# A two-layer recurrent kernel: routing by batch, up products in three fp32r passes, the scan's left operand by DMA

## The chip, the cores and the metric

The kernel runs on one core of a Trainium2 chip. The metric is the device time of one execution in microseconds (us), the median of several runs. Five engines work side by side: TensorE (PE, weight loads shown as PEld), VectorE (DVE), ScalarE (ACT), GpSimd (POOL) and SyncE (SP), which issues all DMAs here. Order between engines is kept by semaphores that the program names.

## The reference, cut to what matters

The input x is 4 batches x 512 tokens x 128 channels, all in fp32. Layer 0 normalises it (LayerNorm), computes a linear attention branch and a mixture-of-experts branch, multiplies the two (silu of the second) and adds the product to x. Layer 1 does the same with a pairwise scan as its attention branch and a second mixture of experts.

```python
# layer 0 gate: 32 experts in 4 groups, 2 groups stay, 8 experts taken
scores = sigmoid(logits); choice = scores + bias
group score = sum of the two best in a group; mask = the 2 best groups
topk_idx = top 8 of where(mask, choice, 0); w = scores[topk]; w = w / (w.sum + 1e-20) * 2.5
# layer 1 scan over tokens, d = 1, 2, 4, ..., 256
shifted = concat([identity] * d, x[:, :-d])
v = (shifted + x) @ W                       # W = polar factor of W_scan_raw
att = softmax(q k^T / sqrt(32)) over 4 lanes per token, q = shifted, k = x
x = shifted + rms_norm(att @ v) / (1 + lane)
# layer 1 experts: 8 of width 512, 2 taken
relu(x @ w1[e] + b1[e]) @ w2[e] + b2[e]
```

## The kernel before, in words

Every engine has one program, written out by hand, and instructions of an engine run in its order. Tokens lie on partitions (token layout, 4 tiles of 128 tokens per batch) or channels do (channel layout, 128 x 512 per batch).

Prologue. VectorE does LayerNorm (`layer_norm` L1123, `normalise` L1135), TensorE transposes to channels and makes the router's logits for all 16 token tiles, ScalarE copies `xnT` and a rounded `xnT_hi` out and takes the sigmoid (L924). GpSimd splits the gate and up weights of layer 0 into two fp32r parts (`split_weights` L368) and makes the remainder `xnT_lo` (L373). VectorE routes all 16 tiles in one chain of small steps (L1160 to L1224): MAX8 per group, comparisons of group scores, MAX8 and match-replace, weights, and three bf16 parts of them (`gate0_parts`). TensorE transposes these (`gates_to_rows` L609) for all batches, then the loop begins.

Layer 0 loop. For each batch b and each pair p of experts (16 pairs), TensorE does `gate_up` (L583: six fp32r passes of 512 columns, high x low, high x high, low x high, for gate and for up), `gate_rows` (one bf16 product that spreads the gates), `down` of two pairs earlier (fp32), and `extras` (L689): attention products, the steps of a polar iteration that makes W, the transposes of layer 1's input. VectorE does `routed_hidden` (L1226, two multiplications, L1230 and L1235) and its `extras` (L1291), among them `polar_step`, `attention_stats` at p = 11, `gate_tokens` at p = 4. `h0` is a ring of three.

Crossing. VectorE finishes layer 0 for batch 3 and normalises it, TensorE transposes it, does `scan_input` (L682), then `router_logits` (L744, layer 1, all tiles), then `values` of the first slot. VectorE does `routing1` (L1321) behind its first slot.

Scan. 9 levels x 4 batches = 36 slots, k = 0 to 35. In each slot:
- TensorE: `state_channels` of the next slot (L767, 4 transposes of x_tok), `values` (L783, (left + x) W), the first half of `expert_down` of one block of layer 1's experts, `left_tokens` of the next slot (L775, 4 transposes), the second half, and four `expert_up` products of the next block (L792, fp32, 512 columns each, with w1 loaded from memory per expert). Bank 3 serves up products 0 and 3.
- ScalarE: `state_in` (L1019, copies the state in channel layout into xT, which has 256 columns of the identity ahead of it, and from there a copy shifted by d columns, leftT), `values_out`, `left_out` (L1027, from bank 1 to left_tok), `expo`, `square`, four `relu`, `rsqrt`.
- VectorE: `products` (L1357, left from bank 1), `scores` (L1369), `add_lanes` (L1363), `score_max`, `softmax_shift`, four accumulations of expert output (L1404), `square_sum` (L1383), `exp_sum`, `mix_values` (L1392).
- GpSimd: `halve_mix` (L469), `rms_factor` (L477), `scale_z` (L481), `new_state` (L488, writes x_tok of two slots back), `sum_inputs` (L444, leftT + xT of the next slot), `last_product` (L451), `last_mix` (L460).
SyncE loads w1 and w2 of the next expert behind semaphores.

Tail. In slot 33 TensorE also does `gated_biases` (L750); then come the last slots, the gating of the state, projections and the output.

## Time and profile before

| what | value |
|---|---|
| median of 3 runs | 631.2 us (624.67 to 637.21) |
| the profiled execution, its own time | 631.67 us |
| its span (first to last instruction) | 630.0 us |
| TensorE busy / VectorE / ScalarE / GpSimd | 563.2 / 507.2 / 282.2 / 377.2 us |
| mean granted TensorE clock | 0.95 |
| HBM traffic | 9.50 MB read, 1.05 MB written |

Times in rows are microseconds from the span's start. An instruction's row gives its start, its duration, its engine and line, what it writes and reads, and in brackets how long its engine had been idle and what ended that. TensorE rows of an fp32 product come in two entries each. PEclk is the granted TensorE clock, 1.00 being full speed. Lines L524 and L527 are TensorE's helpers for a product and a transpose.

### The profile page before, as it was taken

To read this page: it belongs to the slowest core of one execution; us is meant where nothing else is said; L and a number is where in the kernel's file an instruction comes from. 1 tells how busy PE (TensorE), PEld (TensorE's weight loads), DVE (VectorE), ACT (ScalarE), POOL (GpSimd) and SP (SyncE) were. 2 spreads that over 40 slices of the span, in tenths; PEclk is the share of its full clock that TensorE was granted. 3 is DMA by queue.
4 is the path that set the end of the run, shared out by engine and by line. 5 is a ranking of instruction groups with operands and counts; after the bars stand their busy time and mean duration, and the time that the engine had idled before them with its cause. 6 is when DMAs were issued, how large, how long until landed. Compare 5 with 4: busy or idle time off the path is not lost.

```text
span 630.0 us, 9276 instructions
## 1 busy us (share of the span) xinstructions
PE 563.2 (89%) x2934; PEld 405.8 (64%) x2934; DVE 507.2 (81%) x922; ACT 282.2 (45%) x640; POOL 377.2 (60%) x347
## 2 busy tenths in 40 slices
PE   4949999999999995889999999999999999997854
PEld 3735666666666664767767667667677676675724
DVE  7584565664765764599999999999999999999775
ACT  3612242242252244154654655645645546555332
POOL 6930010030030033339999998998999999989754
PEclk9987999999999998689999999999999999999677
DMA  8300000000000000000100000010000100000002
GB/s 255 116 2 0 2 0 2 0 1 0 2 0 2 2 0 0 1 1 2 34 0 17 17 8 25 0 33 0 17 17 0 33 0 17 17 1 0 2 0 68
DMA packets 12185, 10.87 MB, mean 17 GB/s; under 512 B 1784, under 2 KB 10624, under 8 KB 11776
## 3 DMA queue, kind: packets, MB, share of 16 engines
q1 hardware_dynamic: 12160, 10.55, 5.4%
q8 instruction: 13, 0.21, 0.1%
q14 instruction: 12, 0.10, 0.1%
HBM read 9.50 MB, written 1.05 MB: 17 GB/s over the span
## 4 chain that ended last, share of the span: by engine, by line
DVE 38%; PE 36%; issue 17%; ACT 5%; POOL 2%; DMA 0%; DVEq 0%; ACTq 0%; POOLq 0%
PE bank L524 34%; DVE bank L1369 10%; DVE shared L1357 9%; DVE shared L1363 7%; ACT shared L1043 3%; PE bank L527 2%; DVE shared L1392 2%; DVE shared L1377 1%; DVE ssum L1387 1%; DVE smax L1373 1%; POOL shared L469 1%; ACT shared L1041 1%; DVE z_ms L1383 1%; DVE shared L1404 1%; DVE ln_stats L1126 1%
## 5 line engine op out<-in xcount | busy, mean ns | idle before, releaser
L524 PE MATMUL bank<-xnT,w 128*128 128x512 f32 x256 | 121.1, 608 | 5.6 <-ACT shared L1055 5.6
L524 PE MATMUL bank<-w,shared 128*128 128x128 f32 x1024 | 125.1, 275 | 0.0
L524 PEld LDWEIGHTS bank<-w,shared 128*128 128x128 f32 x1024 | 119.9, 193 | 0.0
L469 POOL TENSOR_TENSOR shared<-shared 128x1024 f32<-128x1024 f32 x36 | 85.3, 2368 | 25.9 <-DVE shared L1392 25.8
L524 PE MATMUL bank<-shared 128*128 128x512 f32 (+3 forms) x280 | 89.3, 444 | 0.0
L1230 DVE TENSOR_TENSOR shared<-shared,bank 128x512 f32<-128x512 f32 x64 | 44.0, 687 | 55.9 <-PE bank L524 49.5
L935 ACT ACTIVATE shared<-bank 128x512 f32<-128x512 f32 x68 | 40.5, 598 | 97.6 <-PE bank L524 93.4
L1369 DVE TENSOR_REDUCE bank<-shared 128x64 f32<-128x2048 f32 x36 | 82.6, 2295 | 1.2
L524 PEld LDWEIGHTS bank<-xnT,w 128*128 128x128 f32 x256 | 43.9, 192 | 59.6 <-issue 35.5
L1055 ACT ACTIVATE shared<-bank,b_now 128x512 f32<-128x512 f32 x128 | 80.5, 679 | 1.4 <-ACT b_now L1073 1.2
L444 POOL TENSOR_TENSOR shared<-shared,xT 128x512 f32<-128x512 f32 x36 | 60.1, 1670 | 17.7 <-ACT shared L1025 17.7
L524 PE MATMUL bank<-xnT_lo,wgu_hi 128*128 128x512 f32 x136 | 63.7, 468 | 2.8 <-DVE xT L1158 2.8
L524 PEld LDWEIGHTS bank<-shared 128*128 128x128 f32 x280 | 51.2, 198 | 22.6 <-issue 17.3
L1357 DVE TENSOR_TENSOR shared<-bank,x_tok 128x1536 f32<-128x1536 f32 x36 | 63.1, 1752 | 2.9 <-ACT shared L1029 2.7
L1392 DVE TENSOR_TENSOR shared<-shared,bank 128x1536 f32<-128x1536 f32 x36 | 62.8, 1745 | 0.0
L524 PE MATMUL bank<-polar_x,shared 128*128 128x128 f32 x288 | 44.4, 302 | 20.4 <-DVE shared L1392 19.6
L1363 DVE TENSOR_TENSOR shared<-shared 128x512 f32<-128x512 f32 x36 | 60.6, 1682 | 0.4 <-POOL shared L469 0.4
L524 PEld LDWEIGHTS bank<-polar_x,shared 128*128 128x128 f32 x288 | 38.7, 208 | 27.3 <-issue 27.3
L524 PE MATMUL bank<-xnT_hi,wgu_lo 128*128 128x512 f32 x136 | 54.1, 398 | 0.0
L524 PE MATMUL bank<-xnT_hi,wgu_hi 128*128 128x512 f32 x136 | 53.7, 395 | 0.0
L416 POOL TENSOR_SCALAR xn<-x,ln_mv,ln_rstd 128x128 f32<-128x128 f32 x12 | 9.4, 793 | 66.3 <-ACT ln_rstd L888 66.3
L451 POOL TENSOR_TENSOR shared<-shared,x_tok 128x512 f32<-128x512 f32 x36 | 45.6, 1268 | 5.5 <-ACT shared L1029 5.5
(179 smaller groups left out, 915.4 us busy)
## 6 DMA issues: line engine op xcount, KB each, us to landing
w<-in_w SPq DMA_DIRECT2D x32, 64.0 KB, 1.8
w<-in_w SPq DMA_DIRECT2D x8, 256.0 KB, 2.7
shared<-in_wd SPq DMA_DIRECT2D x1, 1088.0 KB, 12.5
x<-in_x SPq DMA_DIRECT2D x4, 256.0 KB, 3.5
shared<-in_wg SPq DMA_DIRECT2D x1, 1024.0 KB, 8.2
shared<-in_wu SPq DMA_DIRECT2D x1, 1024.0 KB, 10.2
out<-x SPq DMA_DIRECT2D x4, 256.0 KB, 2.3
shared<-in_attn_w SPq DMA_DIRECT2D x1, 384.0 KB, 3.7
```

The costliest lines, as they stand in the source:

```text
L444: g.tensor_tensor(sumT[:, b], leftT[:, b], xT[:, b, PAD:PAD + N], ALU.add).then_inc(s("sum_done"), 1)
L451: g.tensor_tensor(prod[:, b % 2, :, :, LANES - 1], left_tok[:, b].rearrange("p j (l d) -> p j l d", l=LANES), x_tok[:, b, :, (LANES - 1) * ...
L469: g.tensor_tensor(mix2[:, b % 2].rearrange("p j l m d -> p (j l) (m d)"), mix[:, b % 2, :, :, 0:2].rearrange("p j l m d -> p (j l) (m d)") ...
L524: return nc.tensor.matmul(out, lhsT, rhs, start=start, stop=stop)
L935: a.activation(silu_g[:, i % 2], bank[G[i % 2]][:], ACT.Silu).then_inc(s("silu_done"), 1)
L1043: a.activation(z_sq[:, b % 2, :, :, 0:LD], z[:, b % 2].rearrange("p j (l d) -> p j l d", l=LANES), ACT.Square).then_inc(s("zsq_done"), 1)
L1055: a.activation(hT[:, c], bank[UP[c]][:], ACT.Relu, bias=b1_now[:, c:c + 1]).then_inc(s("ffn_relu"), 1)
L1230: tt(silu_gu[:, i % 2], silu_g[:, i % 2], bank[U[i % 2]][:], ALU.mult).then_inc(s("gu_done"), 1)
L1357: tt(prod[:, b % 2, :, :, 0:LANES - 1], left.broadcast_to([P, TB, LANES, LANES - 1, LD]), right.broadcast_to([P, TB, LANES, LANES - 1, LD] ...
L1363: tt(z[:, b % 2].rearrange("p j (l d) -> p (j l) d", l=LANES), m[:, :, 0], m[:, :, 1], ALU.add).then_inc(s("z_done"), 1)
L1369: v.tensor_reduce(score[:, b % 2], prod[:, b % 2], AX_X, ALU.add).then_inc(s("score_done"), 1)
L1392: tt(mix[:, b % 2, :, :, 0:LANES - 1], sexp[:, b % 2, :, :, 0:LANES - 1].unsqueeze(4).broadcast_to([P, TB, LANES, LANES - 1, LD]), values. ...
```

## The change

Routing by batch. ScalarE takes exp(-logits) instead of the sigmoid; VectorE adds 1 and takes the reciprocal. The chain stands in four functions for one batch: `route_groups`, `route_masks`, `route_best`, `route_weights`, 20 steps. Batch 0 goes ahead of the loop, mixed with the shared expert's products; batch b + 1 goes into the loop of batch b at p = 3, 7, 9 and 10, its gates are transposed at p = 13. The loads of the first four units of wg and wu go ahead of the attention weights, and GpSimd splits them first. The shared expert's first two blocks on TensorE go ahead of the token sums.

Up products. w1 of all experts is loaded in one DMA into the room of the layer 0 weights once these are split. GpSimd splits it expert by expert (`split_expert`) into the units of `wgu_hi` and `wgu_lo` that the last batch has used; ScalarE makes `xnT_hi` of layer 1's input, GpSimd the remainder (`token_rest1`). `expert_up` is three fp32r passes. VectorE's and GpSimd's scan waits until all eight experts are split. w2 has two buffers.

Scan. x_tok becomes tiles 1 to 4 of `state_ext`, whose tile 0 is the identity. SyncE moves the state down by d tokens into left_tok with two DMAs per slot (`shift`). `sum_inputs` adds left_tok and x_tok in token layout; TensorE transposes the sum (`sum_channels`, between up products 1 and 2), ScalarE copies it out (`sum_in`, between `rsqrt` and `relu` 2). `left_out` copies left_tok into bank 1 for `products`. `state_channels`, `left_tokens`, `state_in` and the padding of xT are gone. The loops over levels on TensorE, ScalarE, GpSimd and SyncE are written out.

```diff
+            sp.dma_start(polar_x[:], scan_raw_d).then_inc(s("ld_scan"), 16)
+            sp.dma_start(wg[:, 1:5], wg_d[:, 1:5]).then_inc(s("ld_next"), 16)
+            sp.dma_start(wu[:, 1:5], wu_d[:, 1:5]).then_inc(s("ld_next"), 16)
...
+            sp.wait_ge(s("w_lo_done"), 6)
+            sp.dma_start(w1, w1_d.rearrange("e p (u m) h -> p e u m h", m=2)).then_inc(s("ld_w1"), 16)
+            def shift(k):
+                b, d = k % B, 1 << k // B
+                sp.wait_ge(s("xtok_done"), k + 1)
+                if d < P:
+                    sp.dma_start(left_tok[d:P, b], state_ext[0:P - d, b, 1:TB + 1]).then_inc(s(f"ld_left{b}"), 16)
+                    sp.dma_start(left_tok[0:d, b], state_ext[P - d:P, b, 0:TB]).then_inc(s(f"ld_left{b}"), 16)
+                else:
+                    j = d // P
+                    sp.dma_start(left_tok[:, b, 0:j], state_ext[:, b, 0:1].broadcast_to([P, j, P])).then_inc(s(f"ld_left{b}"), 16)
+                    sp.dma_start(left_tok[:, b, j:TB], state_ext[:, b, 1:TB + 1 - j]).then_inc(s(f"ld_left{b}"), 16)
+            for k in range(LEVELS * B):
+                shift(k)
...
+            def split_expert(e):
+                if e > 0:
+                    pool.wait_ge(s("u_mm"), item((B - 1) * PAIRS + 2 * e) + 1)
+                units = slice(2 * e, 2 * e + 2)
+                raw = w1[:, e].rearrange("p u m h -> p m u h")
+                g.tensor_copy(wgu_hi[:, :, units], raw).then_inc(s("w1_hi_done"), 1)
+                pool.wait_ge(s("w1_hi_done"), e + 1)
+                g.tensor_tensor(wgu_lo[:, :, units], raw, wgu_hi[:, :, units], ALU.subtract).then_inc(s("w1_lo_done"), 1)
             for b in range(B):
                 state_product(b)
+                if b > 1:
+                    token_rest1(b - 2)
                 if b > 0:
                     add_to_x(b - 1)
                     normalise1(b - 1)
                 attention_tokens(b)
+            token_rest1(B - 2)
+            pool.wait_ge(s("ld_w1"), 16)
+            pool.wait_ge(s("u_mm"), item((B - 1) * PAIRS) + 1)
+            for e in range(E1):
+                split_expert(e)
             pool.wait_ge(s("x1_done"), B)
             g.memset(ecmp[:], 0.0).then_inc(s("ecmp_zero"), 1)
             g.memset(acc[:], 0.0).then_inc(s("acc_zero"), 1)
...
+            token_rest1(B - 1)
+            pool.wait_ge(s("w1_lo_done"), E1)
             sum_inputs(0, 0)
             last_product(0, 0)
...
             def sum_inputs(k, b):
-                pool.wait_ge(s("leftT_cp"), k + 1)
-                g.tensor_tensor(sumT[:, b], leftT[:, b], xT[:, b, PAD:PAD + N],
-                                ALU.add).then_inc(s("sum_done"), 1)
+                pool.wait_ge(s(f"ld_left{b}"), 32 * (k // B + 1))
+                pool.wait_ge(s("xtok_done"), k + 1)
+                after(pool, s("state_mm"), k - 1)
+                g.tensor_tensor(sum_tok[:, b % 2], left_tok[:, b], x_tok[:, b], ALU.add).then_inc(s("sum_done"), 1)
...
             def expert_up(e, blk, c):
-                if blk == 0:
-                    pe.wait_ge(s(f"ld_w1_{c}"), e * 16 + 16)
+                if c == 0:
+                    pe.wait_ge(s("x1lo_done"), blk + 1)
+                    pe.wait_ge(s("w1_lo_done"), e + 1)
                 if c == HC - 1:
                     pe.wait_ge(s("ffn_relu"), (e * B + blk) * HC + 1)
-                mm(bank[UP[c]][:], w1[:, c], xnT[:, blk * N:(blk + 1) * N]).then_inc(s("ffn_up"), 1)
+                u, m = 2 * e + c // 2, c % 2
+                tokens = slice(blk * N, (blk + 1) * N)
+                mm(bank[UP[c]][:], wgu_hi[:, m, u], xnT_lo[:, tokens], True, False)
+                mm(bank[UP[c]][:], wgu_hi[:, m, u], xnT_hi[:, tokens], False, False)
+                mm(bank[UP[c]][:], wgu_lo[:, m, u], xnT_hi[:, tokens], False, True).then_inc(s("ffn_up"), 1)
...
             def slot(k, b, this=True, ahead=True, up=None, down=None, then=None):
-                if ahead:
-                    state_channels(k + 1, (b + 1) % B)
                 if this:
                     values(k, b)
                 if down:
-                    expert_down(*down, range(0, TB // 2))
-                if ahead:
-                    left_tokens(k + 1, (b + 1) % B)
-                if down:
-                    expert_down(*down, range(TB // 2, TB))
+                    expert_down(*down, range(TB))
                 if then:
                     then()
                 if up:
-                    for c in range(HC):
-                        expert_up(*up, c)
+                    expert_up(*up, 0)
+                    expert_up(*up, 1)
+                if ahead:
+                    sum_channels(k + 1, (b + 1) % B)
+                if up:
+                    expert_up(*up, 2)
+                    expert_up(*up, 3)
...
-            state_channels(0, 0)
             silu_y_tokens(B - 1)
             tokens_to_channels(B - 1, GB)
-            left_tokens(0, 0)
             scan_input(B - 1, AT)
+            sum_channels(0, 0)
             router_logits()
             slot(0, 0, up=(0, 0))
...
             def left_out(k, b):
-                act.wait_ge(s("left_mm"), k + 1)
-                a.copy(left_tok[:, b].rearrange("p j c -> p (j c)"), bank[1][:]).then_inc(s("left_tok_cp"), 1)
+                act.wait_ge(s(f"ld_left{b}"), 32 * (k // B + 1))
+                after(act, s("prod_done"), k)
+                a.copy(bank[1][:], left_tok[:, b].rearrange("p j c -> p (j c)")).then_inc(s("left_tok_cp"), 1)
...
+            route_groups(0)
+            route_masks(0)
             dve.wait_ge(s("polar_r_done"), 2)
             ts(polar_x[:], polar_x[:], polar_r[:], None, ALU.mult).then_inc(s("polar_x0"), 1)
+            shared_hidden(0)
+            route_best(0)
+            shared_hidden(1)
+            route_weights(0)
...
+                elif p == 3 and b < B - 1:
+                    route_groups(b + 1)
+                elif p == 7 and b < B - 1:
+                    route_masks(b + 1)
+                elif p == 9 and b < B - 1:
+                    route_best(b + 1)
+                elif p == 10 and b < B - 1:
+                    route_weights(b + 1)
...
+            dve.wait_ge(s("w1_lo_done"), E1)
             slot(0, 0, before=False)
             routing1()
```

## Rows read from the trace of the kernel before

**Rows 1.** windows: PE, PEld, DVE, ACT, POOL busy us, then PEclk, DMA share, GB/s.

```profile
34.00:40.00 6.00, 3.20 (x13) 2.37 (x13) 5.90 (x53) 1.20 (x2) 3.79 (x11) 1.00 0.01 3
46.00:56.00 10.00, 8.23 (x25) 4.71 (x24) 4.07 (x7) 2.72 (x5) 0.00 (x0) 0.52 0.00 0
249.00:262.00 13.00, 13.00 (x62) 12.78 (x63) 4.50 (x4) 2.96 (x5) 1.64 (x2) 0.50 0.00 1
350.00:400.00 50.00, 47.75 (x297) 35.71 (x298) 48.92 (x62) 29.11 (x72) 45.99 (x36) 1.00 0.03 10
```

**Rows 2.** timeline of one scan slot: start us, us, engine line op, [idle before it].

```profile
407.45 1.75 DVE L1357 TENSOR_TENSOR shared<-bank,x_tok 128x1536 f32<-128x1536 f32 x1
...
407.61 2.37 POOL L469 TENSOR_TENSOR shared<-shared 128x1024 f32<-128x1024 f32 x1 [0.65 <-DVE shared L1392]
...
411.37 1.27 POOL L488 TENSOR_TENSOR x_tok<-shared 128x512 f32<-128x512 f32 x1
411.44 1.74 DVE L1363 TENSOR_TENSOR shared<-shared 128x512 f32<-128x512 f32 x1
...
412.66 3.72 PE L524 MATMUL bank<-xnT,w 128*128 128x512 f32 x8
...
417.06 1.75 DVE L1357 TENSOR_TENSOR shared<-bank,x_tok 128x1536 f32<-128x1536 f32 x1
```

**Rows 3.** source view of L1363: duration ns min/median/max, first and last start.

```profile
L1363 DVE TENSOR_TENSOR shared<-shared x36: 681/1744/1761, 277.0 to 615.8; 128x512 f32<-128x512 f32 x36
```

**Rows 4.** timeline, layer 0 loop, batch 0, TensorE and VectorE.

```profile
62.03 0.39 PE L524 MATMUL bank<-xnT_hi,wgu_lo 128*128 128x512 f32 x1
...
62.26 0.39 PE L524 MATMUL bank<-xnT_lo,wgu_hi 128*128 128x512 f32 x1
...
78.98 0.69 DVE L1230 TENSOR_TENSOR shared<-shared,bank 128x512 f32<-128x512 f32 x1 [1.15 <-PE bank L524]
...
79.71 0.69 DVE L1235 TENSOR_TENSOR shared<-shared,bank 128x512 f32<-128x512 f32 x1
...
80.31 0.28 DVE L1283 COPY polar_x<-bank 128x128 f32<-128x128 f32 x1
...
85.20 0.31 PEld L524 LDWEIGHTS bank<-shared 128*128 128x128 f32 x2 [0.55 <-DVE shared L1276]
```

**Rows 5.** DMA issues: KB each, median us to landing.

```profile
w<-in_w SPq DMA_DIRECT2D x32, 64.0 KB, 1.8
w<-in_w SPq DMA_DIRECT2D x8, 256.0 KB, 2.7
```

**Rows 6.** timeline, prologue: GpSimd, VectorE and TensorE.

```profile
24.44 2.35 POOL L369 CAST wgu_hi<-shared 128x2048 fp32r<-128x2048 f32 x1
25.07 4.45 DVE L1165 MAX8 shared<-shared 128x8 f32<-128x8 f32 x64
...
26.87 4.63 POOL L371 TENSOR_TENSOR wgu_lo<-shared,wgu_hi 128x2048 fp32r<-128x2048 f32 x1
...
30.96 0.62 DVE L1170 TENSOR_SCALAR polar_x<-polar_x,polar_r 128x128 f32<-128x128 f32 x1
...
45.30 1.09 PE L527 MATMUL bank<-ident_bf,shared 128*96 128x128 bf16 x8 [5.76 <-DVE shared L1224]
...
48.45 0.61 PE L524 MATMUL bank<-gate0T,pair_row 96*128 96x512 bf16 x1 [0.67 <-ACT gate0T L996]
```

**Rows 7.** timeline, crossing from layer 0 into the scan.

```profile
235.34 1.28 POOL L427 TENSOR_TENSOR shared<-shared 128x512 f32<-128x512 f32 x1
...
252.50 6.83 PE L524 MATMUL bank<-gate_w,xnT 128*128 128x8 f32 x32
...
260.07 1.92 PE L524 MATMUL bank<-polar_x,shared 128*128 128x128 f32 x8
...
273.00 1.76 DVE L1357 TENSOR_TENSOR shared<-bank,x_tok 128x1536 f32<-128x1536 f32 x1 [0.22 <-DVE gate L1349]
```

**Rows 8.** timeline, tail: TensorE.

```profile
588.08 7.19 PE L524 MATMUL bank<-b,shared 8*128 8x128 f32 x32 [2.21 <-ACT shared L1015]
```

388 lines of the change are left out of this document (203 added, 185 removed).

## The prediction

> **What bounds the kernel now.** I read the table of windows first, then one stretch of the timeline for each limit it shows. Through the scan stage the vector engine is busy 48.92 of 50 us and TensorE 47.75 [rows 1], so busy shares alone don't say which of them decides. The timeline of one slot does [rows 2]. A slot is one batch's step in one scan level: `products` starts at 407.45 and the next one at 417.06, a period of 9.61 us, and there are 36 slots, 346 us of the 630. The reader is to see where VectorE stands still while it is counted as busy: `add_lanes` (L1363) lasts 1.74 us in the slot, with a fastest of 0.681 and a median of 1.744 over its 36 [rows 3]. It starts at 411.44, 0.07 us behind GpSimd's `new_state` (411.37, 1.27 us), and ends 0.54 us after that ends: it is held until GpSimd is through. So the loop that sets the period goes `mix_values` end (407.5), GpSimd's `halve_mix` to `new_state` (407.61 to 412.64), the 0.5 us that `add_lanes` really needs, then VectorE alone up to the end of the next `mix_values`. The Trainium skill has this in SBUF — State Buffer, section on the shared port: a VectorE instruction with two SBUF inputs and a GpSimd instruction that reads SBUF exclude one another for a whole instruction, and a tensor-scalar form in a two-port mode meets any GpSimd instruction; by that rule the new GpSimd work below costs VectorE too, and the trace agrees (1.744 against 0.681).
>
> The rest of the span: a prologue to 48.45, a layer 0 loop of 4 batches bound by TensorE (about 48.7 us each), a crossing into the scan up to 273.00, and a tail from 588 on.
>
> **Scan slots.** The change takes from TensorE the four transposes of the left operand and swaps each up product for three fp32r passes. In layer 0 such passes start 0.23 us apart [rows 4], three cost 0.69; the fp32 up products take 3.72 us for four with a wait in it [rows 2], some 0.86 each. That is 4 x 0.17 + 0.45 = 1.1 us of TensorE per slot. ScalarE loses two copies and gains one. None of these stands in the loop above. VectorE's program in a slot is unchanged, and GpSimd's six operations are the same in number and size: `sum_inputs` adds two 128x512 tiles in another layout. GpSimd has 0.65 us idle in the slot in any case. I take 0 per slot.
>
> What must hold for the 0: (a) The left operand now comes by two DMAs, started when `new_state` ends (5.2 us into a slot). The copy into PSUM that needs it may be as late as 1.75 us into the next slot, or even some 5 us before `expo` behind it suffers: 6.2 us of cover, 10 at the outside. Loads of 256 KB landed in 2.7 us [rows 5]; no DMA from SBUF to SBUF is in the trace. From 1.8 (64 KB) to twice 2.7 plus two issues it fits; I take 3.5, hidden, and if it took 8 us the slot would grow by 1 to 2. (b) TensorE now waits for `sum_inputs` in the middle of its slot, with up products 2 and 3 behind it: it would stand about 1 us there (6.3 to 7.3 us in), do the transposes and end near 8.8 to 9.3, before the next `mix_values`. (c) ScalarE does `relu` 2 and 3 some 0.6 us later, to 1.2 us into the next slot, when TensorE is just through `values`. (d) The clock: the row of 46 to 56 at 0.52 follows 5.76 us of idleness [rows 6], and in 34 to 40 it kept 1.00 with 3.20 us busy of 6 [rows 1]. With 7.9 of 9.6 us busy I expect 1.00, the upper of its two levels (2.4 GHz; 0.50 is 1.2).
>
> **Prologue.** The router now works for one batch instead of four ahead of the loop: 16 MAX8 instead of 64 (4.45 us, so 1.1) [rows 6], and the 512-wide steps become 128-wide, 0.2 to 0.3 each by the 0.28 us copy [rows 4]. The exp instead of the sigmoid spares a table load. But GpSimd splits weights up to about 32 us, with subtractions as long as 4.63, and VectorE's small steps stop behind them as the polar scaling did (0.62, to 31.58, when the subtraction ended at 31.50) [rows 6]; before, the 64 MAX8 covered that. Step by step: exp at 22.9, first three steps held until 26.8, MAX8 to 28.2, group masks caught by the second subtraction until 32.1 and done at 33.4, shared products and the other steps to 40.9; then TensorE has `gate_up`, `key_values`, `gate_up` and four transposes to do, and the loop begins near 45.2 instead of 48.45 [rows 6]: 3.2 us. TensorE has no 5.76 us gap any more [rows 6], so that the stretch 46 to 56 at clock 0.52 [rows 1] mostly runs at full rate: about 2 to 3 us more, if no new gap is long enough. I take -5.2; ends +2 (held at every step, clock low) and -9.
>
> **Layer 0 loop.** Routing of batches 1 to 3 moves into batches 0 to 2, at p = 3, 7, 9, 10. Sum per batch on VectorE: 1.9 (groups), 1.5 (masks), 1.6 (best), 2.2 (weights: nine steps of 0.25). VectorE has slack of 1.15 us per pair (its wait before 78.98), and the ring on top. The first three bursts fit. The last doesn't: after `h0` at 79.71 to 80.40 it moves the `polar_x` copy from 80.31 to 82.6, the next pair's products to 83, and the batch-norm and polar steps of p = 11 behind them; TensorE already waits 0.55 us for that polar step (85.20) [rows 4]. I get 1.7 us of wait per batch, 5.1, plus 3 x 0.45 for the gate transposes that now stand in the loop: +6.5. Ends: +1.4 (all hidden) and +12 (each burst costs its 1.5 us excess).
>
> **Crossing into the scan.** This is the largest term. The up products need w1 split into two fp32r parts, for 8 experts, on GpSimd, and the program puts this behind `attention_tokens` of batch 3, which ends at 236.6 [rows 7]. A cast of 2048 columns took 2.35 and a subtraction 4.63 [rows 6], so 512 columns cost 0.65 and 1.25, with the handshakes 2.1 per expert, 16.9 us for 8. Then GpSimd's order is: one activation remainder (to 238.7), the eight splits (255.6), some 2 us given away to VectorE's layer norm, the memsets (2.75), the last remainder (1.3), and only then `sum_inputs` 0 and with it TensorE's first transposes, near 263. In the old kernel that addition was long done, and TensorE did `router_logits` from 252.50, 6.83 us at clock 0.50, and ended `values` at 262 [rows 1, 7]. Now `router_logits` stands behind the transposes: 264 to 271, `values` to 273, first `mix_values` to 275.5, `routing1` 7.5 us as before, slot 1 at 282.7 instead of 273.00: +9.6. Ends: +3 (splits at the rate of one 1.27 us operation each) and +14 (each VectorE step held).
>
> **Tail.** In the last level `gated_biases` takes TensorE 7.19 us [rows 8]. The sum's transposes and ScalarE's copy of them now stand between it and `values`, where before there was only the state's transpose: +1.1; ends 0 and +3.
>
> **Sum**, against the profiled execution, 631.7 us (span 630.0, 1.7 around it; the median of the runs shown is 631.2): 631.7 - 5.2 + 6.5 + 0 + 9.6 + 1.1 = 643.7. The ends of the terms give 627 and 663; they won't all fall on one side, so this case's own range is 635 to 654.
>
> **Rivals.**
> Order at the port turned round, the case on the other side: not slower. The 0.07 us between `new_state` and `add_lanes` is all that decides who goes first. If anything lets `add_lanes` go first, it takes 0.68 instead of 1.74, and the slot is bound by GpSimd instead: 9.61 less its idle 0.65, plus the 0.2 us by which `new_state` waits longer, 9.2 us. That is 0.4 x 35 = -14, so 629.7. It decides from a shift of 0.1 us. For it: new ScalarE and DMA traffic. Against it: VectorE's and GpSimd's instructions up to that point are identical, and both start from the same event.
> Splits and bursts cheap: prologue -8, loop +1.4, crossing +3, tail 0: 628. For it: VectorE's small steps may slip between GpSimd's. Against it: the serial order on GpSimd and the 0.62 us row.
> A wait in the slot: the shift lands late, or `relu` 3 holds the down products, or GpSimd's sum meets VectorE elsewhere. 0.4 us per slot are 14 us: 658.
> The clock falls in the scan because TensorE now idles 1.7 us per slot: 7.9 us of work become up to 15, a period of some 14 us: above 780. The row of 34 to 40 at 1.00 speaks against it.
> A rule of the Trainium skill that speaks about this change is in DMA: Bandwidth & Descriptors, on the cost of a transfer: about 2 us fixed plus the bytes over 436 GB/s, so an estimate of 2.6 us for 256 KB. By that the shift is hidden and the sum stands; the 2.7 us row is a load from HBM and agrees, a copy inside SBUF no row here shows.
>
> **How the numbers follow.** Forecast 0.54, port order 0.14, cheap splits 0.14, wait in the slot 0.14, clock 0.04. About 2% is what a measurement of this kernel can tell from no change, so slower begins at 643.8, nearly on the forecast: half of it, plus the last two cases, is 0.45; faster (under 618.6) needs the port order together with the cheap splits, or a gain that I don't see: 0.13; the rest, 0.42, is within 2%. The range of 80% takes in the lower rivals and most of the wait: 624 to 660.
>
> **What would show it.** Right: slot period 9.61 and L1363 at 1.74 in the timeline; the eight splits in one block from about 238 to 256 on GpSimd; TensorE idle until about 263, slot 1 at 282 to 283; the loop's start near 45; TensorE waits of 1 to 2 us near p = 11 and 12 of batches 0 to 2; clock 1.00 in the scan. Wrong: L1363 at 0.68; a copy to PSUM that waits for a DMA; `sum_inputs` 0 before 258; a scan clock under 1.

## The result, and the profile after

The changed kernel takes 639.1 us (median of 4 runs, 638.2 to 639.4); the kernel before took 630.1 in the runs beside it (4 runs, 624.7 to 637.2). The ratio is 1.0141, with a 95% interval of 1.0097 to 1.0186: slower by about 1.4%. The 637.2 is a slow execution, and the ratios here and below compare fast ones only. The profiled execution took 638.2 us, its span is 636.5 us instead of 630.0.

Where the 6.5 us of span come from is read by four marks that both timelines have: the first `h0` of layer 0's loop, its last, the `products` of slot 1, and the `products` of slots 34 and 35. The lengths between them, each a difference of two starts, in us:

| stretch | before | after | difference |
|---|---|---|---|
| start to the first `h0` | 49.16 | 43.92 | -5.24 |
| first to last `h0` | 189.13 | 193.10 | +3.97 |
| last `h0` to slot 1 | 34.71 | 42.73 | +8.02 |
| slot 1 to slot 34 (33 slots) | 317.00 | 317.55 | +0.55 |
| slot 34 to 35 | 14.87 | 13.99 | -0.88 |
| the rest | 25.13 | 25.21 | +0.08 |

Start with the scan, the longest part. The windows of the kernel after, in the same stretches and with the same columns as [rows 1]:

```profile
34.00:40.00 6.00, 4.22 (x17) 2.87 (x17) 5.42 (x25) 2.28 (x4) 1.55 (x6) 1.00 0.82 307
46.00:56.00 10.00, 9.33 (x35) 5.45 (x34) 7.62 (x28) 2.19 (x4) 0.92 (x2) 1.00 0.00 1
249.00:262.00 13.00, 7.29 (x32) 6.60 (x32) 5.09 (x6) 2.87 (x5) 12.41 (x11) 0.50 0.11 35
350.00:400.00 50.00, 42.61 (x300) 36.56 (x299) 48.95 (x62) 24.86 (x64) 46.13 (x38) 1.00 0.12 33
```

In 350 to 400 TensorE is busy 42.61 us instead of 47.75 and ScalarE 24.86 instead of 29.11: the work did leave them, 1.0 and 0.8 us per slot. VectorE (48.95) and GpSimd (46.13) stand as before, and so does the period. The timeline of one slot, which answers [rows 2]:

```profile
405.16 1.75 DVE L1437 TENSOR_TENSOR shared<-bank,state_ext 128x1536 f32<-128x1536 f32 x1
405.32 2.36 POOL L512 TENSOR_TENSOR shared<-shared 128x1024 f32<-128x1024 f32 x1 [0.60 <-DVE shared L1472]
405.39 1.13 PE L569 MATMUL bank<-polar_x,shared 128*128 128x128 f32 x8 [0.85 <-DVE shared L1472]
...
409.06 1.27 POOL L531 TENSOR_TENSOR state_ext<-shared,left_tok 128x512 f32<-128x512 f32 x1
409.14 1.74 DVE L1443 TENSOR_TENSOR shared<-shared 128x512 f32<-128x512 f32 x1
...
410.29 1.75 POOL L488 TENSOR_TENSOR shared<-left_tok,state_ext 128x512 f32<-128x512 f32 x1
...
412.10 0.66 PE L572 MATMUL bank<-ident,shared 128*128 128x128 f32 x4 [0.61 <-POOL shared L488]
...
414.76 1.75 DVE L1437 TENSOR_TENSOR shared<-bank,state_ext 128x1536 f32<-128x1536 f32 x1
```

From one `products` (L1437) to the next are 9.60 us. `new_state` (L531) starts 0.08 us ahead of `add_lanes` (L1443), which lasts 1.74, as in [rows 2]. What is new is how long TensorE stands still: 0.85 us ahead of `values`, where it was 0.48 before, and 0.61 for the sum, where it did not wait. Its time was turned into waiting.

Then the crossing, which answers [rows 7]: GpSimd's splits (the first and last shown, eight casts and eight subtractions in all), its first sum, and TensorE behind it.

```profile
237.07 0.61 POOL L460 CAST wgu_hi<-shared 128x512 fp32r<-128x512 f32 x1
...
251.50 1.27 POOL L462 TENSOR_TENSOR wgu_lo<-shared,wgu_hi 128x512 fp32r<-128x512 f32 x1
...
256.59 1.26 POOL L488 TENSOR_TENSOR shared<-left_tok,state_ext 128x512 f32<-128x512 f32 x1
...
257.90 1.11 PE L572 MATMUL bank<-ident,shared 128*128 128x128 f32 x4 [4.39 <-POOL shared L488]
258.81 6.83 PE L569 MATMUL bank<-gate_w,xnT 128*128 128x8 f32 x32
265.49 2.06 PE L569 MATMUL bank<-polar_x,shared 128*128 128x128 f32 x8
```

The router's 6.83 us were done from 252.50 before [rows 7]; now they begin 6.3 us later, at the same low clock (0.50). Slot 1 begins at 279.75 instead of 273.00.

### The profile page after: what moved, and what is told of

It reads as the page before. It is cut to its first block, busy times and chain, and to the rows that moved or that the text cites. A ratio compares the mean times of both kernels' runs of the same rounds, so it can differ in the third digit from the quotient of the medians.

```text
span 636.5 us, 8860 instructions
## 1 busy us (share of the span) xinstructions
PE 532.1 (84%) x2918; PEld 410.6 (65%) x2918; DVE 525.6 (83%) x993; ACT 261.9 (41%) x607; POOL 397.3 (62%) x367
## 4 chain that ended last, share of the span: by engine, by line
DVE 40%; PE 31%; issue 17%; ACT 5%; POOL 5%; DMA 0%; DVEq 0%; ACTq 0%; POOLq 0%
PE bank L569 30%; DVE shared L1437 9%; DVE bank L1449 9%; DVE shared L1443 7%; ACT shared L1094 3%; DVE shared L1472 2%; PE bank L572 2%; POOL wgu_lo L462 1%; DVE shared L1457 1%; DVE ssum L1467 1%; ACT shared L1092 1%; DVE shared L1302 1%; DVE smax L1453 1%; DVE shared L1307 1%; POOL wgu_hi L460 1%
## 5 line engine op out<-in xcount | busy, mean ns | idle before, releaser
L569 PE MATMUL bank<-xnT_lo,wgu_hi 128*128 128x512 f32 x264 | 121.1, 459 | 8.7 <-ACT shared L1106 6.9
L569 PE MATMUL bank<-w,shared 128*128 128x128 f32 x1024 | 121.1, 277 | 0.0
L569 PE MATMUL bank<-xnT_hi,wgu_lo 128*128 128x512 f32 x264 | 105.7, 400 | 0.0
L569 PE MATMUL bank<-xnT_hi,wgu_hi 128*128 128x512 f32 x264 | 105.3, 399 | 0.0
L1437 DVE TENSOR_TENSOR shared<-bank,state_ext 128x1536 f32<-128x1536 f32 x36 | 63.0, 1750 | 5.4 <-ACT bank L1080 5.1
L569 PEld LDWEIGHTS bank<-xnT_lo,wgu_hi 128*128 128x128 f32 x264 | 50.9, 193 | 19.9 <-ACT shared L1106 8.9
L1088 ACT ACTIVATE shared<-shared 128x64 f32<-128x64 f32 x36 | 9.2, 256 | 130.8 <-DVE shared L1457 130.8
L488 POOL TENSOR_TENSOR shared<-left_tok,state_ext 128x512 f32<-128x512 f32 x36 | 61.6, 1712 | 0.0
L572 PE MATMUL bank<-ident,shared 128*128 128x128 f32 x180 | 32.7, 306 | 34.4 <-POOL shared L488 24.5
L1443 DVE TENSOR_TENSOR shared<-shared 128x512 f32<-128x512 f32 x36 | 59.7, 1658 | 0.3 <-POOL shared L512 0.3
L569 PEld LDWEIGHTS bank<-xnT_hi,wgu_lo 128*128 128x128 f32 x264 | 50.5, 191 | 11.8
```

Source lines behind the costliest of these rows:

```text
L488: g.tensor_tensor(sum_tok[:, b % 2], left_tok[:, b], x_tok[:, b], ALU.add).then_inc(s("sum_done"), 1)
L569: return nc.tensor.matmul(out, lhsT, rhs, start=start, stop=stop)
L572: return nc.tensor.transpose(out, in_, ident[:] if idm is None else idm)
L1437: tt(prod[:, b % 2, :, :, 0:LANES - 1], left.broadcast_to([P, TB, LANES, LANES - 1, LD]), right.broadcast_to([P, TB, LANES, LANES - 1, LD] ...
L1443: tt(z[:, b % 2].rearrange("p j (l d) -> p (j l) d", l=LANES), m[:, :, 0], m[:, :, 1], ALU.add).then_inc(s("z_done"), 1)
```

## The experiments

Twelve kernels ran. Eleven are made from the kernel after and one from the kernel before. All are read by the same marks (us; "slots" is slot 1 to slot 34):

| kernel | first `h0` | loop | crossing | slots | slot 34 | span |
|---|---|---|---|---|---|---|
| before | 49.16 | 189.13 | 34.71 | 317.00 | 14.87 | 630.0 |
| after | 43.92 | 193.10 | 42.73 | 317.55 | 13.99 | 636.5 |
| 1 fp32 up products | 44.03 | 192.80 | 38.92 | 317.73 | 13.43 | 632.2 |
| 2 router first | 43.25 | 194.41 | 39.03 | 316.29 | 15.31 | 633.3 |
| 3 port order | 43.69 | 193.15 | 42.75 | 307.34 | 15.31 | 627.2 |
| 4 sum on TensorE | 43.99 | 193.13 | 36.45 | 316.97 | 18.17 | 633.5 |
| 5 both of 3 and 4 | 45.49 | 194.32 | 36.42 | 302.82 | 15.37 | 620.6 |
| 6 routing spread | 43.55 | 191.66 | 42.73 | 317.46 | 14.21 | 634.9 |
| 7 splits early | 45.26 | 193.57 | 37.82 | 316.67 | 14.90 | 633.5 |
| 8 all five | 45.51 | 192.00 | 37.70 | 301.21 | 16.91 | 618.1 |
| 9 alternating sums | 43.95 | 190.76 | 34.72 | 296.03 | 15.03 | 605.7 |
| 10 before, port order | 48.96 | 189.35 | 34.71 | 305.66 | 13.96 | 617.9 |
| 11 shift twice | 43.98 | 193.14 | 42.74 | 316.26 | 15.25 | 636.4 |
| 12 as 9, tail spread | 43.90 | 190.78 | 34.73 | 296.12 | 10.82 | 601.6 |

**1. The up products in fp32 again.** The slot period tests what TensorE's time is worth, the crossing what the splits cost.

```diff
-            for e in range(E1):
-                split_expert(e)
...
-                mm(bank[UP[c]][:], wgu_hi[:, m, u], xnT_lo[:, tokens], True, False)
-                mm(bank[UP[c]][:], wgu_hi[:, m, u], xnT_hi[:, tokens], False, False)
-                mm(bank[UP[c]][:], wgu_lo[:, m, u], xnT_hi[:, tokens], False, True).then_inc(s("ffn_up"), 1)
+                mm(bank[UP[c]][:], h_shared[:, e % 4, c * P:(c + 1) * P], xnT[:, tokens]).then_inc(s("ffn_up"), 1)
```

> The up products of layer 1 go back to one fp32 product each, from unsplit weights; the splits of weights and activations are gone, everything else of the change stays. Theory (the slot is held by the loop between VectorE and GpSimd at their shared port; the splits are the crossing's cost): slot period 9.61 us unchanged although TensorE has about 0.7 us more per slot and its idle time before the values shrinks from 0.84 us; the first transposes of the scan start about 9 to 12 us earlier than 257.9 us, the span is 625 to 629 us instead of 636.5. Rival A (TensorE decides the slot, and the fp32r passes pay there): the period grows by 0.3 to 0.7 us, 10 to 25 us over 36 slots, which eats the gain of the crossing, span 635 to 650 us. Rival B (the crossing is set by program order on TensorE, not by the splits): the crossing stays, span 635 to 638 us.

Measured: ratio to before 1.0114 (1.0068 to 1.0160). The period is 9.61 still. The crossing fell by 3.8 us, not by 9 to 12. Its timeline says why:

```profile
245.22 1.27 POOL L486 TENSOR_TENSOR shared<-left_tok,state_ext 128x512 f32<-128x512 f32 x1
...
245.93 4.32 DVE L1181 TENSOR_SCALAR xn<-x,ln_mv,ln_rstd 128x128 f32<-128x128 f32 x4 [0.64 <-ACT ln_rstd L929]
...
250.30 1.12 PE L568 MATMUL bank<-ident,xn 128*128 128x128 f32 x4 [9.25 <-DVE xn L1181]
...
253.96 1.06 PE L568 MATMUL bank<-ident,shared 128*128 128x128 f32 x4
254.82 6.83 PE L565 MATMUL bank<-gate_w,xnT 128*128 128x8 f32 x32
```

GpSimd is ready with its sum at 246.5, but now its four additions and products meet VectorE's `normalise`, which takes 4.32 us. It had been held in the kernel after too, by the splits (3.76 us), and took 1.47 in the kernel before. TensorE gets its first transpose of this stretch at 250.30, even later than the 249.65 of the kernel after, and the scan's first transposes stand behind it in program order. So the splits, with the remainders that go with them, are worth 3.8 us of the crossing's 8.0, and fp32r brought the slot nothing: both that I held of the slot and that the crossing was all splits were put to one test, and only the first stood. The span of 632.2 us is outside the 625 to 629 that was expected.

**2. The router's products ahead of the first transposes.**

```diff
-            sum_channels(0, 0)
             router_logits()
+            sum_channels(0, 0)
```

> TensorE does the router's products of layer 1 before the first transposes of the scan instead of behind them. Theory: the 4.39 us in which TensorE stands idle for the sum take most of the 6.83 us of router products; the slot-1 products start 3.5 to 4.5 us earlier than 279.75 us, span 632 to 633 us. Rival (the router's products are then done at the low clock and the first slot is late by as much, or routing on VectorE sets the time anyway): 636 to 637 us, no difference.

Measured: ratio 1.0088 (1.0051 to 1.0124); crossing -3.7. Slot 1 itself began 3.1 us earlier, short of the 3.5 to 4.5 expected, since the loop took 1.3 us more here. The order on TensorE is worth as much as the splits are; both act on the same idle 4.39 us. Slot 34, whose program is untouched, was 15.31 instead of 13.99; of that below.

**3. VectorE first at the port.**

```diff
             def new_state(k, b):
                 pool.wait_ge(s("zn_done"), k + 1)
+                pool.wait_ge(s("z_done"), min(k + 2, LEVELS * B))
```

> GpSimd's new_state of slot k-2 waits until VectorE's add_lanes of slot k-1 is done, so that VectorE goes first at the shared port. Theory: add_lanes takes 0.68 us instead of 1.74, new_state starts about 0.8 us later, sum_inputs behind it is no longer held and takes 1.3 instead of 1.75 us, GpSimd's idle 0.6 us before halve_mix goes to nearly 0.1: period 9.3 to 9.5 us, span 626 to 633 us. Rival G (GpSimd's own work sets the slot): new_state's wait adds to the period, 9.8 to 10.4 us, span 643 to 665 us. Rival V (add_lanes lasts 1.74 us for its own sake, not because it is held): period 9.61 plus the wait, and add_lanes stays at 1.74.

Measured: 629.7 us, ratio 1.0022 (0.9988 to 1.0057), so no different from the kernel before, and 9.3 us of span less than the kernel after. The period is 9.33.

```profile
404.35 1.05 POOL L524 TENSOR_TENSOR shared<-shared,z_r 128x512 f32<-128x512 f32 x1
404.56 1.38 DVE L1444 TENSOR_TENSOR shared<-shared 128x512 f32<-128x512 f32 x1
...
406.08 1.29 POOL L532 TENSOR_TENSOR state_ext<-shared,left_tok 128x512 f32<-128x512 f32 x1 [0.69 <-DVE shared L1444]
...
407.33 1.29 POOL L488 TENSOR_TENSOR shared<-left_tok,state_ext 128x512 f32<-128x512 f32 x1
```

`sum_inputs` takes 1.29 instead of 1.75 and `halve_mix` no longer waits, as expected. `add_lanes` did not come to 0.68: VectorE is now ahead in time and meets the operation before, `scale_z`, which ends at 405.40; `add_lanes` ends 0.54 us later, at 405.94. That is the same 0.54 by which it ended behind `new_state` in [rows 2]. Now GpSimd is the bound: its only idle time in the slot is the 0.69 of the new wait.

**4. The sum on TensorE.**

```diff
-                    sum_inputs(k + 1, (b + 1) % B)
...
-                    last = tr(bank[0][:, j * P:(j + 1) * P], sum_tok[:, b % 2, j])
+                    out = bank[0][:, j * P:(j + 1) * P]
+                    mm(out, left_tok[:, b, j], ident[:], True, False)
+                    last = mm(out, x_tok[:, b, j], ident[:], False, True)
```

> The sum of the left operand and the state is no longer made by GpSimd: TensorE multiplies both by the identity and accumulates them in one bank, 8 products of 128 columns per slot instead of 4 transposes. GpSimd loses its longest but one operation of a slot (1.75 us), TensorE gains about 0.5 us. Theory (the loop mix_values, halve_mix to new_state, add_lanes, mix_values sets the period, and GpSimd's sum stands outside it): period 9.61 us unchanged, only the first slot about 1 to 2 us earlier, span 634 to 636.5 us. Rival G (GpSimd's total of 9.0 us sets it): period 8.5 to 9.2 us, span 600 to 622 us. Rival P (TensorE sets it): period 9.9 to 10.1 us, span 646 to 654 us.

Measured: ratio 1.0093 (1.0059 to 1.0126); the period is 9.61 to the last digit.

```profile
402.25 1.27 POOL L531 TENSOR_TENSOR state_ext<-shared,left_tok 128x512 f32<-128x512 f32 x1
402.33 1.74 DVE L1446 TENSOR_TENSOR shared<-shared 128x512 f32<-128x512 f32 x1
...
408.11 2.36 POOL L512 TENSOR_TENSOR shared<-shared 128x1024 f32<-128x1024 f32 x1 [1.85 <-DVE shared L1475]
```

GpSimd lost an operation of 1.75 us and now waits 1.85 us instead of 0.60 ahead of `halve_mix`. The race at the port (0.08 us) is unchanged, and so is the time. With 1 this settles the slot: neither TensorE's work nor GpSimd's total sets it, the loop through the port does (experiment 3 is the positive test). Three sizes were off. First, the crossing fell by 6.3 us and not by 1 to 2. The window over the router's products here, with the router's row, then the window over them in the kernel after (the third number from the end is PEclk):

```profile
256.00:261.00 5.00, 5.00 (x40) 5.00 (x39) 3.33 (x4) 0.58 (x1) 3.19 (x3) 0.82 0.13 35
256.32 4.24 PE L567 MATMUL bank<-gate_w,xnT 128*128 128x8 f32 x32
```

```profile
258.00:266.00 8.00, 8.00 (x38) 8.00 (x39) 2.74 (x3) 0.58 (x1) 3.57 (x3) 0.50 0.18 58
```

The router began 2.6 us earlier, counted from the last `h0`, since it no longer waits for GpSimd's sum. It also took 4.24 us instead of 6.83, another 2.6: TensorE's clock was 0.82 over them and not 0.50, so most ran at the upper level. TensorE had not stood still since 251.54 here, where the kernel after has the idle 4.39 us just ahead. That alone is not the reason: in experiment 2 nothing is waited for just ahead of them either, and they take 6.83. What stands between here is the sum, 2.9 us of products. The last 1.1 us is one step less of `routing1` held at the port. Second, TensorE got more to do than the 0.5 us I gave it: products of this kind start 0.22 us apart, so eight take some 1.7 us against 0.4 for the transposes, 1.3 more; I had taken each of a product's two entries for a product. Third, slot 34 grew from 13.99 to 18.17 us and took back two thirds of the crossing's gain: `gated_biases` took 7.19 us instead of 5.69, and the eight products behind it, at the low clock too, 3.8 us where four transposes took 1.1.

**5. Both together.**

> Both earlier edits of the slot together: VectorE's add_lanes goes first at the port, and TensorE makes the sum of left and right. Theory: with the order turned, GpSimd's own chain sets the slot (it stood idle only in its wait, period 9.33 us); with its sum gone as well it needs 9.33 - 1.29 = 8.0 us, TensorE needs 8.4, and VectorE with add_lanes at 0.68 needs 8.55 to 8.7: period 8.6 to 8.9 us, 27 to 35 us less over 35 slots than with 9.61; against the 636.5 us of the changed kernel minus the 3 us that the sum on TensorE gave, span 598 to 612 us. Rival G (the loop through GpSimd decides whatever GpSimd's other work is): 9.33 us again, span 624 to 627 us. Rival P (TensorE decides once the others are shorter): 9.2 to 9.6 us, span 620 to 634 us.

Measured: 619.8 us, ratio 0.9857 (0.9800 to 0.9914); period 9.18, rival P's. Windows of TensorE, PEld, VectorE, ScalarE, GpSimd, and VectorE's waits in a slot:

```profile
400.00:450.00 50.00, 50.00 (x373) 46.74 (x372) 45.55 (x71) 28.03 (x68) 39.01 (x34) 1.00 0.12 36
```

```profile
409.37 0.68 DVE L1447 TENSOR_TENSOR shared<-shared 128x512 f32<-128x512 f32 x1
...
410.20 1.28 POOL L532 TENSOR_TENSOR state_ext<-shared,left_tok 128x512 f32<-128x512 f32 x1 [0.97 <-DVE shared L1447]
410.71 0.35 DVE L1488 SCALAR_TENSOR_TENSOR shared<-bank,gate_now,shared 128x128 f32<-128x128 f32 x1 [0.52 <-PE bank L568]
```

`add_lanes` is free at 0.68, and now VectorE waits for TensorE's down products: TensorE, busy 50.00 of 50 us, is the bound.

**6. Routing in smaller pieces.** The bursts at p = 3, 7, 9, 10 become eight pieces at p = 1, 3, 5, 7, 8, 9, 10 and 12, and the gates are transposed at p = 14:

```diff
-                elif p == 3 and b < B - 1:
+                elif p == 1 and b < B - 1:
                     route_groups(b + 1)
+                elif p == 3 and b < B - 1:
+                    route_top(b + 1, range(0, 2))
...
+                elif p == 5 and b < B - 1:
+                    route_top(b + 1, range(2, TB))
```

> The routing of the next batch is cut into eight pieces of 0.5 to 1.5 us (at p = 1, 3, 5, 7, 8, 9, 10, 12) instead of four of 1.5 to 2.6 us (at p = 3, 7, 9, 10), and the gates are transposed at p = 14 instead of 13. Theory (a burst longer than VectorE's 1.15 us of slack per pair delays TensorE): the steps of +1.5, +1.06 and +1.05 us at p = 3 and of +1.26 at p = 10 go to under 0.5 each, layer 0 ends 3 to 5 us earlier than 240.97 us, span 631.5 to 633.5 us. Rival (VectorE has no room in the loop at all, each microsecond of routing is a microsecond of time): the loop stays at +6 us, span 636 to 637 us. Rival (the handshakes of more pieces cost): later than now.

Measured: ratio 1.0135 (1.0076 to 1.0195); the loop is 1.4 us shorter, not 3 to 5. That number mixes two things. The starts of all 64 `h0`, compared one by one with the kernel before, show what routing costs from the fourth pair on: 3.3 us up to batch 3, where the kernel after loses 6.0. Some 1.2 us were lost again in the first pairs, where TensorE's clock was 0.72 (44 to 50 us) instead of 1.00; experiment 9, with the same routing program and 1.00 there, loses 3.2 and its loop is 2.3 shorter. The pieces up to p = 10 cost nothing that lasts, the 1.5 us at p = 1 with its reciprocal of 0.95 included. What is left, 1.8, 0.75 and 0.75 us in the three batches, comes behind p = 12, at the last piece and the gates' transposes. So the theory holds for the bursts and not for the end of the chain.

**7. Five splits inside layer 0**, where GpSimd waits.

```diff
                     add_to_x(b - 1)
+                    if b == B - 1:
+                        pool.wait_ge(s("ld_w1"), 16)
+                        pool.wait_ge(s("u_mm"), item((B - 1) * PAIRS) + 1)
+                        for e in range(5):
+                            split_expert(e)
                     normalise1(b - 1)
...
-            for e in range(E1):
+            for e in range(5, E1):
                 split_expert(e)
```

> Five of the eight splits of the expert weights are done on GpSimd in layer 0, batch 3, between add_to_x and normalise1, where it waits for about 24 us; three stay in the crossing. Theory (the block of splits on GpSimd is the crossing's cost): five times 1.9 us leave the crossing, the first transposes of the scan start 7 to 9 us earlier than 257.9 us if nothing else is late, at least the layer norm's and the last activation remainder's chain lets 5 us through; layer 0 itself grows by 0 to 1.5 us because VectorE's instructions are held by the splits; span 630 to 633 us. Rival (the crossing is set by the router's products and routing on VectorE): less than 1.5 us gained, span 635 to 637 us.

Measured: ratio 1.0104 (1.0042 to 1.0165). The crossing is 4.9 us shorter and the loop 0.5 longer, but the prologue, whose program is untouched, took 1.3 us more; the first transposes started at 254.78, 3.1 us earlier and not 5 to 9. The crossing gained 1.1 us more than in 1, where all splits are gone: here the first sum comes behind `normalise`, which takes 1.11 us and is not held.

**8. All five edits.**

> All five edits together: VectorE first at the port, the sum on TensorE, the router's products ahead of the first transposes, routing in smaller pieces, five splits inside layer 0. Theory: slot period 8.6 to 8.9 us; layer 0 -3 to -5 us, crossing -6 to -9 us (the last edits overlap there, since they fill the same idle time of TensorE): span 588 to 604 us, 4 to 7% under the kernel before. Rival (the gains of the crossing are one and the same wait): the crossing gives only 3 to 4 us, span 594 to 606 us. Rival (period stays at 9.33 or above): span over 612 us.

Measured: 618.8 us, ratio 0.9842 (0.9796 to 0.9889). The period is 9.18 as in 5, so the range was missed; the third case has the span but not its reason. The crossing is 37.70, where 5, without the other three edits, had 36.42: with the sum on TensorE the router's products ahead of it are a loss. There is no wait left for them to fill, and they are back at 6.83 us at the low clock (0.50 in 252 to 259), where they took 4.38 in 5 behind the sum. Edits that gained 3.7, 4.9 and 6.3 us alone gave 5.0 together.

**9. Alternating sums**: 3, 6 and 7, with the sum on TensorE for batches 0 and 2 and on GpSimd for 1 and 3.

```diff
-                    sum_inputs(k + 1, (b + 1) % B)
+                    if (b + 1) % B % 2:
+                        sum_inputs(k + 1, (b + 1) % B)
```

> VectorE first at the port, the sum on TensorE for batches 0 and 2 and on GpSimd for batches 1 and 3, routing in smaller pieces, five splits in layer 0; the router's products stay behind the first transposes. Theory: with all sums on GpSimd that engine sets the slot (9.33 us), with all on TensorE that one does (50.00 of 50 us busy, 9.18 us). With half on each, GpSimd needs (9.33 + 8.04) / 2 = 8.7 us and TensorE 9.18 - 0.65 = 8.5 us on average, VectorE 8.55: two slots together take 17.2 to 18.0 us instead of 18.36, 6 to 18 us less than all five edits, span 600 to 612 us. Rival (slots don't even out, each pays its own longest engine): 9.2 us on average, span 614 to 620 us.

Measured: 609.3 us, ratio 0.9683 (0.9652 to 0.9713). Slots take 8.81 and 9.17 in turn, 8.99 on average. The crossing is back at 34.72, as long as in the kernel before, but by another way: the router's products took 4.07 us here (clock 0.84 in 252 to 257) and 6.83 there, so 2.8 of the 8.0 us came from the clock. It is 3.0 us shorter than in 8, where the router stands first.

**10. The one wait, in the kernel before.**

> The kernel before, with only the one wait: new_state of slot k-2 behind add_lanes of slot k-1. Theory (the slot's period is the port's, not the change's): it gains as the changed kernel did: 9.3 to 9.5 us instead of 9.61, 4 to 10 us, span 620 to 626 us against 630.0; TensorE, busy 47.74 of 50 us, needs 9.18 and so doesn't stop it. Rival (in the kernel before TensorE and ScalarE sit closer and another wait takes over): 9.6 us or more, span 629 to 636 us.

Measured: 618.0 us, ratio 0.9827 (0.9763 to 0.9892); slots of 9.24 to 9.29, a little less than expected, and 12.1 us of span less. `add_lanes` took 0.68 us in slot 2 and grew slot by slot to 1.42 in slot 20: VectorE, now the faster of the two, runs ahead until it meets `scale_z`, and GpSimd's round sets the period throughout. The loop at the port is the kernel's, not the change's; one wait pays here more than the change costs.

**11. The shift twice.**

```diff
+                    sp.dma_start(spare[:, 0:2], state_ext[:, b, 1:3]).then_inc(s(f"ld_left{b}"), 16)
+                    sp.dma_start(spare[:, 2:TB], state_ext[:, b, 3:TB + 1]).then_inc(s(f"ld_left{b}"), 16)
```

> From level 2 on each shift is preceded by two DMAs of the same total size into a place that nobody reads, and the readers of the left operand wait for all four: a shift that moves 512 KB and takes four issues. Theory (the shift is covered): the copy into PSUM on ScalarE waits for a DMA by 1 to 4 us, but the products of that slot come over 7 us behind its present place, so the period stays 9.61 us to within 0.1; span 636 to 640 us. Rival (ScalarE's in-order queue hands the wait on to expo, or GpSimd's sum waits for it and GpSimd hands it on): period 10.0 to 12 us, span 650 to 710 us.

Measured: 638.3 us (2 runs), ratio 1.0139 (1.0092 to 1.0185); period 9.62. The source view of ScalarE's copy of the left operand says what it waited for (us, times), first with the shift doubled, then in the kernel after:

```profile
  DVE shared L1441: 6.4, 28
  DMA left_tok<-state_ext: 6.2, 4
```

```profile
  DVE shared L1437: 6.3, 27
  DMA left_tok<-state_ext: 1.3, 4
```

Of the 28 slots with a doubled shift, in 22 it is there before VectorE has freed the bank, and in the last two the copy doesn't wait at all. In four the copy waits for the DMA, 1.4 to 2.0 us each and 6.2 in all instead of 1.3, and the period doesn't feel it. They are the same four in both kernels, those of the level with d = 4. In the kernel after the worst of them landed 6.8 us behind the end of `new_state` (the copy at 369.11), so the shift can take twice the 3.5 us that I had taken for it.

**12. The tail spread.** As 9, with the gates of batches 0 to 2 turned one slot earlier, and the bias products half in slot 33 and half in slot 34.

```diff
-            slot((LEVELS - 1) * B + 1, 1, then=gated_biases)
-            slot((LEVELS - 1) * B + 2, 2)
+            slot((LEVELS - 1) * B + 1, 1, then=lambda: gated_biases(range(0, 2)))
+            slot((LEVELS - 1) * B + 2, 2, then=lambda: gated_biases(range(2, B)))
```

> As the kernel with alternating sums, and in the last level the gates of batches 0 to 2 are turned one slot earlier, behind the last down products, and the bias products are done for two batches in slot 33 and for two in slot 34, instead of all in slot 33 (counting from 0). Theory (gated_biases delays the sum's transposes and values behind it on TensorE, 16 transposes and 32 products in one block of 9 to 10 us): the slot of 15.03 us goes to 10 to 11.5 us (its four additions of 2.47 us in all stay), the one before it grows from 8.55 to 8.6 to 9.5 us: span 601 to 604 us against 605.7. Rival (the block is late for another reason, as the low clock of TensorE in the tail): 605 to 607 us.

Measured: 603.9 us (603.2 to 606.2), ratio 0.9597 (0.9544 to 0.9650). Slot 34 is 10.82 instead of 15.03 and slot 33 is 8.53. This version beats both kernels, by 4.0% and by about 5.5% (603.9 against 639.1).

## Why the prediction was right or wrong

The forecast was 643.7 us, the profiled execution took 638.2 and the median is 639.1. It is within the range (624 to 660) and slower, by the mechanisms that were named, but the size is about half: the terms add up to +12.0 us of span, and +6.5 were measured. The 1.4% also lies under the 2% from which the prediction counted a result as slower; it gave 0.42 to a difference within 2%. No single step turned the result; four of the terms were too high by 0.5 to 2.3 us each, and the two that stand right at first sight, prologue and loop, do so partly by luck, as shown below.

**Slots, 0: right, and shown.** The period is 9.61 before and after; experiments 1, 4 and 11 load or relieve TensorE, GpSimd and the DMA and don't move it, 3 and 10 turn the order at the port and do. The shift was slower than I took it (up to 6.8 us instead of 3.5), and a copy into PSUM did wait for a DMA, four times and 1.3 us in all, which the prediction names as a sign of being wrong; it stayed hidden. The Trainium skill (SBUF — State Buffer, section SBUF: two separate sides) says that whoever starts first gets the shared port for a whole instruction; experiment 3 agrees, since `add_lanes` ended 0.54 us behind `scale_z` there, and 0.54 behind `new_state` before. The 0.55 us in the table are two differences at the start: slot 1 is 0.9 us shorter (8.56 instead of 9.44), and slot 2 is 1.45 longer (11.07 instead of 9.62), with VectorE waiting 1.36 us for TensorE's down products at a granted clock of 0.82 and 0.84 (280 to 290 and 290 to 300 us) instead of 1.00 (a scan clock under 1 was another sign that I had named). In experiment 2, with 1.00 there, slot 2 takes 9.62.

**The port rival: its price was right by luck, its trigger wrong.** It put the turned order at a period of 9.2; one wait in the kernel before gives 9.24 to 9.29. It took off GpSimd's idle 0.65 us and added 0.2 for `new_state`'s wait. That wait is 0.69 us, and `sum_inputs`, no longer held, gives back some 0.45 (1.28 instead of 1.72); the two omissions cancel. `add_lanes` at 0.68 for good was wrong as well: it meets `scale_z` instead and takes 1.4. And the change's new traffic on ScalarE and the DMA queue didn't shift a race of 0.07 us: both engines still start from the same event, and it stands at 0.07 to 0.09 in all but the last slots. Slot 1 is short (8.56 us) for another reason: `new_state` doesn't run in it at all, and the sum and `last_product`, which `add_lanes` met there before (1.57 us), are already done in slot 0.

**The crossing, +9.6: was +8.0; the mechanism half right.** The splits took 1.9 us each and not 2.1, and GpSimd gave away 0.5 us to VectorE's work of this stretch and not 2 (it was VectorE that lost, 2.3 us in `normalise`). `sum_inputs` 0 began at 256.59, before the 258 that I had named as a sign of being wrong, and the first transposes came at 257.90, not near 263; 1.3 us of that is layer 0 ending earlier. What came behind was worse than forecast. `routing1`, which I had left at 7.5 us, took 9.4. Its steps in the kernel before, then in the kernel after with what holds them on GpSimd (L488 is `sum_inputs`, L494 `last_product`):

```profile
266.08 2.38 DVE L1328 TENSOR_TENSOR shared<-logits,lmax 128x128 f32<-128x128 f32 x1
268.39 0.26 DVE L1335 TENSOR_TENSOR shared<-logits 128x112 f32<-128x112 f32 x1
268.57 0.18 DVE L1333 TENSOR_TENSOR shared<-logits 128x16 f32<-128x16 f32 x1
```

```profile
271.00 2.01 DVE L1408 TENSOR_TENSOR shared<-logits,lmax 128x128 f32<-128x128 f32 x1
272.82 1.35 POOL L488 TENSOR_TENSOR shared<-left_tok,state_ext 128x512 f32<-128x512 f32 x1
272.93 1.36 DVE L1415 TENSOR_TENSOR shared<-logits 128x112 f32<-128x112 f32 x1
274.12 1.33 POOL L494 TENSOR_TENSOR shared<-left_tok,state_ext 128x512 f32<-128x512 f32 x1
274.22 1.28 DVE L1413 TENSOR_TENSOR shared<-logits 128x16 f32<-128x16 f32 x1
```

The first step was held in both. The next two are held by the sum and product of slot 2, which in the kernel before waited for ScalarE's copies until `routing1` was over (274.60). So the 8.0 us are 7.6 from the last `h0` to the router's last product, 1.8 in `routing1`, and 1.4 won back between the two, where TensorE no longer has the next slot's transposes to do. What fell is that the splits and what waits for them explain the crossing: taken out they give 3.8 us (experiment 1), the order on TensorE alone gives 3.7 (experiment 2), the sum on TensorE 6.3, of which 2.6 are the clock (experiment 4), and they overlap. Experiment 9 gets back all 8.0, with 2.8 from the clock.

**The prologue, -5.2: was -5.24 at the first `h0`, and -7.5 in all.** The two held steps were there (24.97 and 29.20):

```profile
24.97 1.50 DVE L1217 TENSOR_SCALAR shared<-shared 128x128 f32<-128x128 f32 x1 [6.59 <-ACT shared L966]
26.51 0.95 DVE L1219 RECIPROCAL shared<-shared 128x128 f32<-128x128 f32 x1
...
29.20 2.16 DVE L1231 TENSOR_TENSOR shared<-shared 128x16 f32<-128x16 f32 x1
...
39.22 0.50 PE L569 MATMUL bank<-xnT_lo,wgu_hi 128*128 128x512 f32 x1 [1.78 <-DVE h_shared L1209]
```

But the forecast was 3.2 us by the loop's start and 2 from the clock behind it. The loop began at 43.43, not near 45.2, so 5.0 earlier than before: the shared products were done at 39.76 and not 40.9, and TensorE's work behind them took 3.7 us and not 4.3. The clock's part (1.00 instead of 0.52 in 46 to 56) came on top, 2.3 us within the first four pairs, as forecast. That -5.24 meets -5.2 is luck: the first mark holds only the first of the two parts, and that one was 1.8 us too small.

**The loop, +6.5: was +6.0 (from -7.5 to -1.6 at the first `h0` of batch 3), with its parts wrong.** "The first three bursts fit" failed. The one at p = 3 lasts 2.6 us, since the reciprocal of 128 elements takes 0.95 and not the 0.2 to 0.3 at which I priced any step of 128. The `h0` behind it comes 1.5, 1.1 and 1.1 us late in the three batches; part of that is made up within two pairs, and 0.8, 0.3 and 0.7 us are left by p = 10. The last burst costs 1.26 per batch at p = 11 and not 1.7, and with the gates' transposes 4.2 us in all and not 6.5. So 1.8 us that had been put at nothing stand against 2.3 put too high, and the near hit of the sum is luck too. Experiments 6 and 9 show that smaller pieces take away 2.7 of the 6.0 us and that the rest sits at the end of the chain.

**The tail, +1.1: was -0.9.** The sign is the clock's: `gated_biases` took 5.69 us here instead of the 7.19 of [rows 8], as part of it ran at the upper clock (granted 1.00 up to 597 us, 0.51 behind). In the kernel after and experiments 1, 2, 3, 6, 7 and 11, which have the same tail, slot 34 takes 13.4 to 15.3 us, and each time 8.3 us more than `gated_biases` (5.13 to 7.01). In the kernel before it is 7.7 more (7.19, 14.87), in experiment 10 7.9 more (6.05, 13.96). At the same clock the term is thus +0.4 to +0.6, half of what I took. That the block of products delays the slot, as the term assumed, experiment 12 shows: spread over two slots, it gives 4.2 us.

## What to carry to other kernels

When two engines start from one event and meet at a shared port a few hundredths of a microsecond apart, find out who has slack, and write the order down with a wait: one line gave 1.5 to 1.9% of the span here, more than the three rewritten stages cost. Taking work off an engine pays only if its idle time doesn't grow by the same amount; look at the brackets ahead of the instruction that closes the loop. Once that loop is opened, the next bound is close (9.61, then 9.33 on GpSimd, 9.18 on TensorE, 8.99 in turns), so move work by halves, and don't add up gains measured against the same wait. A gain can also be the clock's: with the sum made on TensorE ahead of them, the router's unchanged products took 2.6 us less, so compare the duration of untouched work before crediting an edit.
